# Transposing the normalised rows of the next batch by VectorE blocks and SBUF transfers instead of by TensorE, in a four-layer residual kernel on one core

## The reference: what is computed

```python
def L0(x, W1, b1, W2, b2, gamma, beta):            # adapter and layer norm
    h = relu(x @ W1 + b1)
    a = x + h @ W2 + b2
    normed = (a - mean(a)) * rsqrt(var(a) + 1e-5)
    return normed * gamma + beta
def L1(x, W, b): return x @ W.T + b                # one 256x256 matrix per batch
def L2(x, ...):                                    # five nets 256 -> 1024 -> 256, gated by row 0
    return expert_out * g0 + s0 * g1 + s1 * g2 + s2 * g3
def L3(x, ...):                                    # masked attention pooling over the 512 rows
    return (softmax(masked scores) @ x) / count
x = x + L0(x); x = x + L1(x); x = x + L2(x); x = x + L3(x)
```

## Time and profile before

| | us |
|---|---|
| median of 3 runs | 507.05 (506.36 to 507.7) |
| the profiled execution | 505.97 |
| its span in the trace | 504.2 |

### The profile page before, as it was taken

How to read it: one execution, slowest core, us unless ns; L and a number is a source line. 1 busy time by engine, 2 the same in 40 slices (tenths; PEclk the granted TensorE clock), 3 DMA queues, 4 the chain that set the end, 5 groups by cost and what they waited for, 6 DMA issues and landing times.

```text
span 504.2 us, 6976 instructions
## 1 busy us (share of the span) xinstructions
PE 496.4 (98%) x2353; PEld 411.8 (82%) x2353; DVE 338.4 (67%) x640; ACT 257.6 (51%) x486; POOL 234.8 (47%) x199
## 2 busy tenths in 40 slices
PE   8999999999999999999999999999999999999995
PEld 5788888888888888888888888888888888888984
DVE  5687226874787787785578697687478778444276
ACT  4655654443556564545356655545355747445233
POOL 1674455445345445444645444544544544744022
PEclk9999999999999999999999999999999999999999
DMA  5965354222264442423137443322222432420002
GB/s 157 194 176 142 113 155 138 83 85 84 85 146 126 110 111 84 142 71 107 59 121 182 99 155 102 126 83 85 83 85 85 110 100 83 162 90 2 1 0 85
DMA packets 77658, 52.99 MB, mean 105 GB/s; under 512 B 40758, under 2 KB 67382, under 8 KB 77622
## 3 DMA queue, kind: packets, MB, share of 16 engines
q1 hardware_dynamic: 75734, 50.44, 34.6%
q10 hardware_dynamic: 1888, 2.10, 1.3%
HBM read 48.33 MB, written 2.10 MB: 100 GB/s over the span
## 4 chain that ended last, share of the span: by engine, by line
PE 95%; DVE 3%; issue 0%; POOL 0%; ACT 0%; DVEq 0%; POOLq 0%
PE ps_hid L843 14%; PE ps_hid L842 14%; PE ps_hid L847 14%; PE ps_net L900 14%; PE ps_net L904 14%; PE ps_net L899 14%; PE ps_net L871 2%; PE ps_net L662 1%; PE ps_side L533 1%; PE ps_side L537 1%; PE ps_side L532 1%; PE ps_side L543 1%; PE ps_side L546 1%; PE ps_hid L683 1%; PE ps_side L730 1%; PE ps_hid L791 0%
## 5 line engine op out<-in xcount | busy, mean ns | idle before, releaser
L1886 POOL TENSOR_TENSOR wi_lo<-raw_wi,wi_hi 128x512 fp32r<-128x512 f32 x78 | 103.3, 1325 | 211.3 <-ACT wo_hi L1085 110.2
L1795 DVE SCALAR_TENSOR_TENSOR hid_lo<-ps_hid,hid_hi 128x512 fp32r<-128x512 f32 x160 | 110.3, 689 | 130.0 <-ACT hid_hi L1106 128.6
L1106 ACT ACTIVATE hid_hi<-ps_hid 128x512 fp32r<-128x512 f32 x160 | 95.4, 597 | 195.7 <-PE ps_hid L847 194.0
L842 PE MATMUL ps_hid<-x2T_hi,wi_lo 128*128 128x512 f32 (+1 forms) x332 | 125.9, 381 | 0.0
L843 PE MATMUL ps_hid<-x2T_hi,wi_hi 128*128 128x512 f32 (+1 forms) x332 | 125.4, 380 | 0.0
L899 PE MATMUL ps_net<-hid_hi,wo_hi 128*128 128x512 f32 x304 | 118.6, 390 | 0.0
L900 PE MATMUL ps_net<-hid_hi,wo_lo 128*128 128x512 f32 x304 | 118.6, 390 | 0.0
L1887 POOL TENSOR_TENSOR wo_lo<-raw_wo,wo_hi 128x512 fp32r<-128x512 f32 x78 | 104.3, 1338 | 0.0
L847 PE MATMUL ps_hid<-x2T_lo,wi_hi 128*128 128x512 f32 (+1 forms) x332 | 99.0, 380 | 0.0
L904 PE MATMUL ps_net<-hid_lo,wo_hi 128*128 128x512 f32 x304 | 94.0, 390 | 0.0
L843 PEld LDWEIGHTS ps_hid<-x2T_hi,wi_hi 128*128 128x128 f32 x332 | 62.5, 188 | 11.7
(11 more groups left out here) (319 smaller groups left out, 490.7 us busy)
## 6 DMA issues: line engine op xcount, KB each, us to landing
raw_wi<-in_L_cond_share_wi_dram SPq DMA_DIRECT2D x23, 512.0 KB, 3.7
raw_wo<-in_L_cond_share_wo_dram SPq DMA_DIRECT2D x23, 512.0 KB, 4.8
raw_wi<-in_L_cond_expert_wi_dram SPq DMA_DIRECT2D x16, 512.0 KB, 3.7
raw_wo<-in_L_cond_expert_wo_dram SPq DMA_DIRECT2D x16, 512.0 KB, 4.9
next_x2T<-in_x_dram SPq DMA_DIRECT2D x24, 64.0 KB, 4.3
x_rows<-in_x_dram SPq DMA_DIRECT2D x3, 512.0 KB, 3.4
x_rows<-netT SPq DMA_DIRECT2D x48, 32.0 KB, 2.0
out_dram<-out_rows SPq DMA_DIRECT2D x5, 256.0 KB, 5.4
```

Of the source, the lines that this page charges most:

```text
L842: mm(dst, wi_lo[:, w, k, c], x2T_hi[:, k, rows], start=(k == 0), stop=False)
L1106: fn(hid_hi[:, ring(b, q)], ps_hid[:, ring(b, q)], ACT.Relu).then_inc(hid_hi_ready, 1)
L1795: v.scalar_tensor_tensor(out=hid_lo[:, ring(b, q)], in0=ps_hid[:, ring(b, q)], scalar=0.0, in1=f32(hid_hi[:, ring(b, q)]), op0=ALU.max, op ...
L1886: g.tensor_tensor(wi_lo[:, w], raw_wi[:, half % 2, :, c], f32(wi_hi[:, w]), ALU.subtract)
```

## The change

TensorE's 24 transposes of `norm` in the loop are gone, and with them the function `normalised` and two steps of TensorE's semaphore. In their place, for each of the three next batches: VectorE transposes the 32x32 blocks of `norm` by two instructions in slot 30, right behind the normalising, into the buffer `x_rows`; SP, at the end of its program for the batch, waits for them and issues 16 transfers that put the blocks into `next_x2T`; and VectorE makes both halves of x1T in slot 34, from SBUF, once all 16 have landed. ScalarE's copy of hi part 0 moves from slot 33 to 34 and that of hi part 1 from 34 to 35. The lo parts stay in slot 35 and the L1 products in 36 and 37. The prologue keeps its TensorE transposes.

```diff
-    A_SLOT = dict(..., xb=31, norm=30, normT=32, x1_hi=33, x1_lo=35, y=36, base=37)
+    A_SLOT = dict(..., xb=31, norm=30, x1T=34, x1_hi=34, x1_lo=35, y=36, base=37)
...
+        norm_blocks, normT = x_rows[:].rearrange("p r d -> p (r d)"), next_x2T[:].rearrange("p k s -> p (k s)")
...
+            def place_norm(i):
+                sp.wait_ge(a_dve.sem, a_dve.at(i, "norm_blocks"))
+                for a in range(P // BK):
+                    for c in range(P // BK):
+                        src = norm_blocks[a * BK:(a + 1) * BK].rearrange("p (n s) -> p n s", s=P)[:, :, c * BK:(c + 1) * BK]
+                        dst = normT[c * BK:(c + 1) * BK].rearrange("p (n s) -> p n s", s=P)[:, :, a * BK:(a + 1) * BK]
+                        sp.dma_start(dst, src).then_inc(norm_in, 16)
...
             def batch(b, first, last):          # the SP program
...
+                if not last:
+                    place_norm(b + 1)
...
-            def normalised(slot, i):            # the TensorE program
-                if 0 <= slot - A_SLOT["normT"] < KD:
-                    k = slot - A_SLOT["normT"]
-                    pe.wait_ge(a_dve.sem, a_dve.at(i, "norm"))
-                    for r in range(R):
-                        last = nc.tensor.transpose(ps_side[:, k, r * P:(r + 1) * P], norm[:, r, k * P:(k + 1) * P], ident[:])
-                    last.then_inc(a_pe.sem, 1)
...
                     last.then_inc(a_dve.sem, 1) # the VectorE program, slot 30
-                if 0 <= slot - A_SLOT["normT"] < KD:
-                    k = slot - A_SLOT["normT"]
-                    dve.wait_ge(a_pe.sem, a_pe.at(i, f"normT{k}"))
-                    here(f"xb{k}")
-                    v.scalar_tensor_tensor(out=x1T[:, k], in0=ps_side[:, k], scalar=gamma[:, k:k + 1], in1=xbT[:, k],
-                                           op0=ALU.mult, op1=ALU.add).then_inc(a_dve.sem, 1)
+                    here("norm")
+                    for k in range(KD):
+                        blocks = norm_blocks.rearrange("p (k r s) -> p k r s", k=KD, s=P)[:, k]
+                        last = v.transpose(blocks, norm[:, :, k * P:(k + 1) * P])
+                    last.then_inc(a_dve.sem, 1)
+                if slot == A_SLOT["x1T"]:
+                    dve.wait_ge(norm_in, 16 * (P // BK) ** 2 * i)
+                    here("xb1")
+                    for k in range(KD):
+                        v.scalar_tensor_tensor(out=x1T[:, k], in0=normT[:, k * S:(k + 1) * S], scalar=gamma[:, k:k + 1], in1=xbT[:, k],
+                                               op0=ALU.mult, op1=ALU.add).then_inc(a_dve.sem, 1)
```

More of the change, by code:

```diff
@@ L59, in cond_resid_program @@
     assert PAIRS % RING == 0 and HALVES % 2 == 0 and HP == 2
-    A_SLOT = dict(w1=20, blocks=20, xT=22, w2=25, subj_blocks=25, hid=26, subj_w=27, adapt=28, stats=29, xb=31, norm=30, normT=32, x1_hi=33, x1_lo=35, y=36, base=37)
+    A_SLOT = dict(w1=20, blocks=20, xT=22, w2=25, subj_blocks=25, hid=26, subj_w=27, adapt=28, stats=29, xb=31, norm=30, x1T=34, x1_hi=34, x1_lo=35, y=36, base=37)
     GATE_SUM = {23: 0, 27: 1, 38: 2}
@@ L252, in cond_resid_program @@
         x0_in = [sem("x0_in0"), sem("x0_in1")]
-        blocks_in, rows_in, x_in, subj_in, subj_b_in, out_stored = sem("blocks_in"), sem("rows_in"), sem("x_in"), sem("subj_in"), sem("subj_b_in"), sem("out_stored")
+        blocks_in, rows_in, norm_in, x_in, subj_in, subj_b_in, out_stored = sem("blocks_in"), sem("rows_in"), sem("norm_in"), sem("x_in"), sem("subj_in"), sem("subj_b_in"), sem("out_stored")
         w1_in, b1_in, b2_in, w2_in, beta_in, gamma_in = sem("w1_in"), sem("b1_in"), sem("b2_in"), sem("w2_in"), sem("beta_in"), sem("gamma_in")
@@ L268, in cond_resid_program @@
         evac_dve = Steps(sem("evac_dve"), "g0 g1 g2 g3")
-        a_pe = Steps(sem("a_pe"), "hid adapt0 adapt1 normT0 normT1 y0 y1", 1)
+        a_pe = Steps(sem("a_pe"), "hid adapt0 adapt1 y0 y1", 1)
         a_act = Steps(sem("a_act"), "xhi0 xhi1 hid_below hid_up subj_w_hi x1hi0 x1hi1", 1)
         a_dve = Steps(sem("a_dve"), "w1_hi xT0 xT1 xlo0 xlo1 w2_hi w2_up b2_hi b2_lo subj_wT hid_sum hid_hi hid_lo subj_w_lo sum0 sum1 stats sums mean var_eps "
-                                    "norm xb0 xb1 x1T0 x1T1 x1lo0 x1lo1 x2T0 x2T1", 1)
+                                    "norm norm_blocks xb0 xb1 x1T0 x1T1 x1lo0 x1lo1 x2T0 x2T1", 1)
         a_pool = Steps(sem("a_pool"), "w1_lo w2_lo rstd", 1)
@@ L917, in batch @@
                         second_product(b, s, first, last)
-                    if not last:
-                        normalised(q, b + 1)
                     if not first:
```

## The result

| | before | changed |
|---|---|---|
| median, us | 506.71 (4 runs) | 527.28 (4 runs, 525.97 to 527.96) |
| ratio | | 1.0397 (1.0375 to 1.0419) |
| the profiled execution, us | 505.97 | 525.97 |
| its span, us | 504.2 | 523.4 |
| granted clock, mean | 0.999 | 0.98 |

What follows compares the result with a forecast made beforehand. TensorE was taken to bound the kernel, with the transfers' issuing on SP deciding the change: 4.76 us a passage, saved transposes included, three times 14.3 us, on a median of 507.05 gives 521.4 us; range 518 to 528.

Steps and rivals of the forecast that it cites:

- TensorE bound, 2.6 us saved: TensorE, busy 98% of the span, sets the time; dropping 24 transposes of `norm` takes 2.6 us off its path.
- The issuing decides: On SP, 16 transfers issued one behind the other take 10.85 us, the last landing 2.0 us after its start, at 120.24.
- The path from the landing to y: Last landing, x1T0, hi parts, lo parts, then y's lo products at 124.27, 4.76 us later than before.
- The stall: TensorE waiting for y's operands behind the transfers: 4.76 us a passage, 14.3 us in three; 63% at full clock.
- Slot 31's delay costs nothing: VectorE's block transposes push slot 31's lo part back 1.3 us; costed at nothing, as VectorE catches up.
- the cover: VectorE's 1.33 us idle ahead of slot 33's lo part; without it slot 31's delay would cost 1.3 us a passage.
- The late weights are hidden: Next batch's first weights, queued on SP behind the transfers, land 4.8 us later, at 124.1, but delay no TensorE work.
- My 2 us to spare: ScalarE splits the late weights by 125.4; its next duty, hid_hi of chunk 37, comes at 127.5.
- The clock: TensorE's clock falls to 1.2 GHz in its 4.0 us wait, costing 2.1 us a fall; 25% for at least one passage.
- my third rival: TensorE's clock falls in the wait: 523.5 us if in one passage, 527.7 in all three; 25% for at least one.
- The rivals on the fast side: Transfers land in time, 504.4 us, 5%; or each issues in 0.317 us as from HBM, 508 us, 5%.

Runs made afterwards that it cites:

- n4: Changed kernel with only the first 4 of the 16 transfers issued and waited for; 504.09 us, 0.9945 of the kernel before.
- best: Changed kernel, next weights issued first, 6 transfers on ScalarE, GpSimd's x3T addition in slot 33, x1T in 35, y in 38; 504.32 us, 0.9947 of before.
- small: Changed kernel with all 16 transfers, each moving one of its 8 runs per partition (4 KB, not 32); 524.09 us, 1.0355 of before.
- q2_late1: Changed kernel with x1T and the steps to y one slot later, ScalarE issuing 6 of the transfers and SP 10; 514.59 us, 1.0155 of before.
- wf: Changed kernel, SP issuing the next batch's first weights ahead of the 16 transfers, slots unchanged; 526.83 us, 1.0389 of before.
- warm: Changed kernel plus 16 TensorE products on zeros ahead of its wait for x1T in slot 36; 522.19 us, 1.03 of before.
- n12: Changed kernel with only 12 of the 16 transfers issued and waited for; 514.1 us, 1.0141 of the kernel before.
- wf_late2_base33: Changed kernel, next weights issued first, x1T through y two slots later, GpSimd's x3T addition moved from slot 37 to 33; 507.17 us, 1.0008 of before.
- before_late2: Kernel before the change, with its transposes, x1T, hi and lo parts and y two slots later; 512.09 us, 1.0103 of before.
- wf_late2: Changed kernel, next batch's first weights issued ahead of the transfers, x1T and all behind it two slots later; 519.75 us, 1.0259 of before.

## Why the prediction was right, and where not

- *TensorE bound, 2.6 us saved.* Right within the intervals: n4 and best measure 2.6 and 2.3 us.
- *The issuing decides.* Right: 10.43 us in the first passage, predicted as 10.85, landing 1.91 as 2.0, and small shows the cost to be the instruction's. The rule of the Trainium skill that it is "usually small relative to the DMA itself" (DMA: Bandwidth & Descriptors, "Issuing engines are not separate DMA queues") does not hold for such a set, whose issuing is over five times its landing; what the section says of saving the issue time by several engines does, as q2_late1 shows. With two queues or fewer transfers the last one lands earlier and the time goes down.
- *The path from the landing to y.* Predicted 124.27 - 120.24 = 4.03 us, measured 123.77 - 119.87 = 3.90. TensorE waited 3.65 us ahead of it, forecast 4.0, but only 0.19 ahead of the lo products and not 1.2, as at half the clock the hi products filled that wait. The stall is 13.3 us for three passages, forecast 14.3.
- *Slot 31's delay costs nothing.* Right as to time. But xbT, pushed beside GpSimd's work, took 3.02 us in the first passage and 1.9 in the others in place of 0.87. In the first it used up the cover: VectorE had no idle time ahead of slot 33's lo part, and it waited 5.86 us for the transfers and not the 6.6 forecast. I had not seen that.
- *The late weights are hidden.* Right for this kernel: ScalarE had to wait 1.2 us for them in slot 36, and wf takes that away and gains nothing. My 2 us to spare were real, but only because the stall was there; with y later they became the largest loss.
- *The clock.* This is the failed step. I gave its fall 25% and took 521.4 us without it as the likeliest; it fell in each of the three passages, so the case that came true is my third rival at its full extent, 527.7, against 527.28, and the range held because it reached up to that rival. That it is so close is partly luck: the stall measured 13.3 us and not 14.3, the clock 5.9 and not 6.3, and some 0.8 us of the loss lie outside the traced span. The price of a fall, 2.1 us from the earlier trace rows, measured 2.0 in the profile, and warm gives 5.1 us for three. In the earlier trace rows only the doubled durations speak for the low clock; the granted clock of the trace is 1.00 there. What I held against the fall, the two pairs of products in the middle of the wait, did not help: in two passages the clock fell before they started, in the other one 0.1 us after. And n12 shows a fall with a longest wait of 2.0 us, half of the 3.9 us of the earlier trace rows.
- *The rivals on the fast side.* Both needed a pitch of issues far below 0.65 us; rows and small exclude them.

## What to carry to other kernels

Many small transfers in a row cost their issuing on the queue, not their bytes: count the instructions, multiply by the issue time of the nearest like them, and add one landing; then look at what stands behind them in that queue. A stall hides other late things, so a fix that only moves the consumer may uncover them; what is late next has to be looked up in each in-order queue, and a wait of TensorE of some us is to be priced with its clock.

## What the hardware showed that I had not expected

- An issue of a 32-partition SBUF to SBUF transfer takes 0.61 us for 32 KB and 0.59 for 4 KB, while one of the same shape from HBM takes 0.32. Why they differ is open.
- The granted clock fell 2.9, 3.8 and 4.3 us after the last product in the three passages of the changed kernel and stayed at 1.2 GHz for 6.8 us each time. In n12 it fell with no wait above 2.0 us, for 3.4 us.
- VectorE instructions with all operands in SBUF took two to three times as long beside GpSimd: xbT, one input and a scalar column, 1.51 us in place of 0.474 (medians of six), the two x1T 3.15 in all in place of 1.41 (first passage of wf_late2_base33), a lo part 1.86 in place of 0.76 (medians of six, in before_late2). For the lo parts an experiment shows the cause: with the addition moved away (wf_late2_base33) they took 1.28 us for the two in the first passage, as against 3.94 in wf_late2. For xbT and x1T it is the reading of the timelines only.
